# A windowed attention block on one core: the last denominators' rows go first, VectorE copies the shift rows, ScalarE issues them later

## The reference

```
h   = layer_norm(x) padded to 28 x 28, cut in 14 x 14 windows (4 an image)
q, k, v = heads of h @ qkv_w + qkv_b              # 12 heads of 16
s   = (q * 16**-0.5) @ k.T + q @ Rh.T (rows) + q @ Rw.T (columns)
o   = softmax(s) @ v;  o = o @ proj_w + proj_b
x2  = x + o                                       # windows put back, padding cut off
h2  = layer_norm(x2)
out = x2 + gelu(h2 @ mlp_w1 + mlp_b1) @ mlp_w2 + mlp_b2
```

## Time and profile before

| | |
|---|---|
| median of 3 runs | 262.92 us (262.45 to 263.22) |
| the profiled execution | 264.93 us, span 263.1 us, mean granted clock 0.981 |
| TensorE busy | 242.9 us (92%), 1996 matmuls |
| weight loads | 189.6 us (72%) |
| VectorE busy | 166.4 us (63%) |
| ScalarE busy | 133.5 us (51%) |
| GpSimd busy | 115.5 us (44%) |
| chain that ended last | PE 61%, DVE 12%, ACT 9%, DMA 8%, issue 3% |

### The profile page before, as it was taken

One profiled execution on the slowest core, in us unless ns is written; L12 is line 12 of the kernel. 1 busy time (PEld: TensorE's weight loads), 2 busy tenths in 40 slices (PEclk: granted clock), 3 DMA queues, 4 the chain that ended last, 5 costly groups with the idle time before them and its releaser, 6 DMA issues.

```text
span 263.1 us, 5440 instructions
## 1 busy us (share of the span) xinstructions
PE 242.9 (92%) x1996; PEld 189.6 (72%) x1996; DVE 166.4 (63%) x453; ACT 133.5 (51%) x240; POOL 115.5 (44%) x180
## 2 busy tenths in 40 slices
PE   7789999999799998999999998949999999999994
PEld 3335578897677776778776765638878889798994
DVE  3997739237878887888879895627996461400010
ACT  2156698336557675676756666520357461604100
POOL 4449775905017665857566772910410490000000
PEclk9999999999799999999999999976999999999999
DMA  5745224786047778676767624371000001000011
GB/s 173 184 110 136 50 58 111 184 200 157 25 116 157 167 183 194 155 170 169 191 165 187 163 54 140 95 235 47 0 2 2 0 0 60 2 30 30 20 43 60
DMA packets 22232, 27.80 MB, mean 106 GB/s; under 512 B 7288, under 2 KB 18410, under 8 KB 22206
## 3 DMA queue, kind: packets, MB, share of 16 engines
q1 hardware_dynamic: 18253, 21.37, 31.0%
q0 software_dynamic: 3424, 5.89, 10.0%
q10 hardware_dynamic: 528, 0.20, 0.3%
HBM read 5.84 MB, written 1.57 MB: 28 GB/s over the span
## 4 chain that ended last, share of the span: by engine, by line
PE 61%; DVE 12%; ACT 9%; DMA 8%; issue 3%; ACTq 2%; POOL 2%; SPq 1%; DVEq 0%; POOLq 0%
PE ps L1472 12%; PE ps L1456 8%; PE ps L1246 6%; PE ps L1312 5%; PE ps L1288 5%; PE ps L1137 5%; DMA kop<-hl 3%; ACT pm L744 3%; DVE bias L931 3%; PE ps L1211 2%; PE ps L1369 2%; PE ps L1356 2%; PE ps L1317 2%; ACTq L724 2%; DMA ot<-osb 2%
## 5 line engine op out<-in xcount | busy, mean ns | idle before, releaser
L950 DVE TENSOR_REDUCE nmax<-ps 98x2 f32<-98x392 f32 x96 | 52.8, 565 | 19.0 <-PE ps L1246 17.3
L744 ACT ACTIVATE pm<-ps 98x784 f32<-98x784 f32 x48 | 39.0, 825 | 16.2 <-PE ps L1288 16.1
L1246 PE MATMUL ps<-kop,qop 126*98 126x196 f32 x192 | 37.3, 279 | 2.3 <-DVE nmax L950 0.9
L1246 PEld LDWEIGHTS ps<-kop,qop 126*98 126x98 f32 x192 | 25.8, 168 | 9.3 <-DVE nmax L950 4.0
L1472 PE MATMUL ps<-w2t,gl 128*128 128x192 f32 x192 | 31.7, 326 | 0.0
L1472 PEld LDWEIGHTS ps<-w2t,gl 128*128 128x128 f32 x192 | 31.4, 190 | 0.3
L816 ACT ACTIVATE gl<-ps,vec 128x512 f32<-128x512 f32 x24 | 16.1, 684 | 29.4 <-PE ps L1456 29.4
L1288 PE MATMUL ps<-qop,kop 128*98 128x196 f32 x192 | 26.6, 262 | 0.0
L1093 DVE TENSOR_TENSOR xn<-ps,xres 128x384 f32<-128x384 f32 x8 | 4.5, 558 | 33.5 <-PE ps L1472 33.5
L955 DVE TENSOR_REDUCE nmax<-ps 120x1 f32<-120x316 f32 x48 | 22.2, 482 | 4.0 <-PE ps L1252 3.0
L1137 PE MATMUL ps<-ht,bias 128*128 128x512 f32 x48 | 21.6, 595 | 2.7 <-DVE ht L866 1.4
(11 more groups left out here) (162 smaller groups left out, 499.1 us busy)
## 6 DMA issues: line engine op xcount, KB each, us to landing
qop<-bias POOLq DMA_DIRECT2D x7, 343.0 KB, 5.7
qop<-hl SPq DMA_DIRECT2D x12, 196.0 KB
kop<-hl SPq DMA_DIRECT2D x12, 196.0 KB
bias<-in_x SPq DMA_DIRECT2D x4, 384.0 KB, 4.6
xres<-in_x SPq DMA_DIRECT2D x4, 384.0 KB, 4.2
out<-xn SPq DMA_DIRECT2D x8, 192.0 KB, 1.9
kop<-kst SPq DMA_DIRECT2D x3, 477.8 KB
ot<-osb POOLq DMA_DIRECT2D x44, 32.0 KB, 2.3
```

The source lines that it names most:

```text
L744: a.activation(pm[0:HALF, gi], ps[0:HALF, b0:b0 + 2, 0:2 * WIN], ACT.Exp).then_inc(s["exp_done"], 1)
L950: v_.tensor_reduce(nmax[0:HALF, h % 2, 2 * n:2 * n + 2], ps[0:HALF, bank, 0:2 * WIN].rearrange("p (t k) -> p t k", t=2), AX.X, ALU.max, ne ...
L1246: o = mm(ps[0:HALF, bank, WIN * t:WIN * (t + 1)], q[0:R_MAX, WIN * n + HALF * t:WIN * n + HALF * (t + 1)], kk[0:R_MAX, WIN * n:WIN * (n + ...
```

## The change

Seven edits:

- SyncE issues the load of the residual's first chunk after the two DMAs of the last denominators' rows, no longer before.
- GpSimd waits for the last reciprocals before it splits the first MLP layer's weights.
- The copies of the shift rows out of PSUM move from ScalarE to VectorE: the main one after the tenth reduction of the head, the rest one after the second reduction of the next head (for the last head after the loop).
- ScalarE keeps only the DMAs of the shift rows, and issues them after the exponentials of groups 3 and 5, no longer before those of groups 3 and 5.
- VectorE forms the last reciprocals before the fourth multiply of heads 0 to 7.
- TensorE's first two projections change places.
- In the second norm's eviction ScalarE does both banks without waiting for VectorE, and VectorE follows it bank by bank; the next transposes wait for VectorE's reads and no longer for its low parts.

```diff
-            load_residual(0)
             sp.wait_ge(s["rden_ready"], 3)
             for l in range(2):
                 sp.dma_start(rd[4 * l:4 * (l + 1), 1].bitcast(F32), den_parts[:, 2, l]).then_inc(s["rd1_in"], 16)
+            load_residual(0)
             load_residual(1)
...
                 pool.wait_ge(*loaded)
+                pool.wait_ge(s["rden_ready"], 3)
                 g.tensor_copy(high[:], w[:]).then_inc(s["w1_split"], 1)
...
-            def main_shifts(h):
-
-                act.wait_ge(s["mt_done"], 2 * h + 1)
-                if h >= 2:
-                    act.wait_ge(shift_in[h % 2], 16 * (h // 2))
-                a.copy(shift[:, h % 2].bitcast(F32R), ps[0:4 * B, score_bank(main_max_use(h)), 0:HALF]).then_inc(s["shift_ready"], 1)
+            def store_main_shifts(h):
+
                 act.wait_ge(s["shift_ready"], 2 * h + 1)
                 act.dma_start(qop[h % RING].bitcast(F32)[R_MAX:ROWS, 0:MAIN], shift[:, h % 2]).then_inc(shift_in[h % 2], 16)
...
-                    if gi == (10 - LEAD) // 2 and h + 1 < HEADS:
-                        main_shifts(h + 1)
-                    if gi == (14 - LEAD) // 2 and h + 1 < HEADS:
-                        rest_shifts(h + 1)
+                    if gi == 3 and h + 1 < HEADS:
+                        store_main_shifts(h + 1)
+                    if gi == 5 and h + 1 < HEADS:
+                        store_rest_shifts(h + 1)
...
                 act.wait_ge(s["tp2_done"], 2 * c + 2)
-                act.wait_ge(s["h2f_ready"], 2 * c + 1)
                 a.activation(h2s[0:C - P, c % 2], ps[0:C - P, 7, :], ACT.Identity, scale=vec[0:C - P, G2B:G2B + 1],
...
+            def main_shifts(h):
+
+                dve.wait_ge(s["mt_done"], 2 * h + 1)
+                if h >= 2:
+                    dve.wait_ge(shift_in[h % 2], 16 * (h // 2))
+                v_.tensor_copy(shift[:, h % 2].bitcast(F32R), ps[0:4 * B, score_bank(main_max_use(h)), 0:HALF]
+                               ).then_inc(s["shift_ready"], 1)
...
                     maxima(h, n)
+                    if n == 1 and h:
+                        rest_shifts(h - 1)
...
                     maxima(h, n)
+                    if n == 9:
+                        main_shifts(h)
...
                     reciprocal_parts(k)
+            rest_shifts(LAST)
...
-            for j in range(4):
+            for j in range(3):
                 normalise(0, j)
             for par in range(2):
                 dve.wait_ge(o_in[par], 5 * 16 * (LAST // 2))
             dve.wait_ge(s["ten_den_in"], 16)
             reciprocal_parts(2)
+            normalise(0, 3)
...
-                dve.wait_ge(s["tp2_done"], 2 * c + 2)
-                v_.tensor_scalar(h2g[:], ps[0:C - P, 7, :], vec[0:C - P, G2B:G2B + 1], vec[0:C - P, B2B:B2B + 1],
-                                 ALU.mult, ALU.add).then_inc(s["h2f_ready"], 1)
                 dve.wait_ge(s["h2h_ready"], 2 * c + 1)
                 v_.tensor_scalar(h2f[:], ps[:, 6, :], vec[:, G2A:G2A + 1], vec[:, B2A:B2A + 1],
+                                 ALU.mult, ALU.add).then_inc(s["h2f_ready"], 1)
+                dve.wait_ge(s["h2h_ready"], 2 * c + 2)
+                v_.tensor_scalar(h2g[:], ps[0:C - P, 7, :], vec[0:C - P, G2B:G2B + 1], vec[0:C - P, B2B:B2B + 1],
                                  ALU.mult, ALU.add).then_inc(s["h2f_ready"], 1)
...
                         elif gi == 4:
+                            projection_of_eight(1)
+                        else:
                             projection_of_eight(0)
-                        else:
-                            projection_of_eight(1)
...
                     pe.wait_ge(s["h2h_ready"], 2 * c)
-                    pe.wait_ge(s["h2l_ready"], 2 * c)
+                    pe.wait_ge(s["h2f_ready"], 2 * c)
```

More of the change, by code:

```diff
@@ L715, in _, with store_rest_shifts @@
                 last_bias_columns(b)
-            def main_shifts(h):
-                act.wait_ge(s["mt_done"], 2 * h + 1)
-                if h >= 2:
-                    act.wait_ge(shift_in[h % 2], 16 * (h // 2))
-                a.copy(shift[:, h % 2].bitcast(F32R), ps[0:4 * B, score_bank(main_max_use(h)), 0:HALF]).then_inc(s["shift_ready"], 1)
+            def store_main_shifts(h):
                 act.wait_ge(s["shift_ready"], 2 * h + 1)
                 act.dma_start(qop[h % RING].bitcast(F32)[R_MAX:ROWS, 0:MAIN], shift[:, h % 2]).then_inc(shift_in[h % 2], 16)
[L726 to L731, removed]
+            def store_rest_shifts(h):
                 act.wait_ge(s["shift_ready"], 2 * h + 2)
@@ L757, in output @@
                 a.copy(osb[:, h % 2], ps[:, 6, :]).then_inc(s["osb_ready"], 1)
-            main_shifts(0)
-            rest_shifts(0)
+            store_main_shifts(0)
+            store_rest_shifts(0)
             a.activation(warm[:, 4:8], warm[:, 0:4], ACT.Exp)
@@ L962, in maxima_parts, with rest_shifts @@
                 v_.tensor_tensor(low.bitcast(F32R), m, high, ALU.subtract).then_inc(s["parts_ready"], 1)
+            def main_shifts(h):
[4 more added lines that the diff above has]
+                               ).then_inc(s["shift_ready"], 1)
+            def rest_shifts(h):
+                dve.wait_ge(s["mt_done"], 2 * h + 2)
+                if h >= 2:
+                    dve.wait_ge(rest_shift_in[h % 2], 16 * (h // 2))
+                v_.tensor_copy(shift_rest[:, h % 2].bitcast(F32R), ps[0:2 * NP, score_bank(rest_max_use(h)), 0:PAIR]
+                               ).then_inc(s["shift_ready"], 1)
             def reciprocal_parts(k):
@@ L1084, in second_channels_lo @@
                 v_.tensor_tensor(h2l[:, c % 2], h2f[:], h2h[:, c % 2], ALU.subtract).then_inc(s["h2l_ready"], 1)
-                dve.wait_ge(s["h2h_ready"], 2 * c + 2)
                 v_.tensor_tensor(h2s[C - P:P, c % 2], h2g[:], h2s[0:C - P, c % 2],
```

## The result

The changed kernel takes 260.53 us (median of 7 runs, 258.71 to 261.9), the kernel before on the same chip 263.22 (7 runs): ratio 0.9893, 95% interval 0.9854 to 0.9932. That is 2.7 us less where 5.4 were forecast. The profiled execution took 261.90 us with a span of 260.1 (264.93 and 263.1 before), mean granted clock 0.974.

The account below looks back on a forecast made before the run. TensorE was taken to lead, pausing 3.3 us for the last denominators, after which the clock fell, and once per head. Denominators 4.1 + heads 1.3 = 5.4 off 262.9 gave 257.5 us; 8 in 10 between 255.9 and 260.9.

Parts of the forecast that it names:

- Denominators: Way of the last denominators to the MLP: 4.1 us saved, 2.2 by earlier rows and 1.9 by the clock.
- the residual's place: Residual's first load issued behind the two stores of rows: price 0, at the other end 1.0 us.
- the splits are hidden: GpSimd's later weight splits end some 5.3 us after 168.0, are read at 192.06, and cost nothing.
- after about 2.4 us: Head 10's denominators, sent off at 164.00, land about 2.4 us later, in time for the earlier reciprocals.
- the 0.9 for the reordering: Last reciprocals before VectorE's fourth multiply of the first eight heads: gain 0.9 us.
- Shift copies, stores: In the heads: VectorE copies 0.25 us each; group 3's exponentials start at 124.41, shift DMA issued under them.
- slower: Rival: later shifts take 3.84 us to landing, each of 11 heads starts weights 0.81 to 0.85 later; 267.8 us, chance 0.07.
- What the heads give: Pauses before group 3's sums, 3.1 us over the heads, of which 1.3 us were counted as arriving.
- the clock should then stay up: After TensorE's pause near 171 us, cut to 1.1 us, the granted clock holds: 1.9 us gained.
- the clock still falls: Rival: clock falls after the 1.1 us pause and thin spread matmuls; 2.2 + 1.3 saved, 259.4 us, chance 0.16.
- threshold of 3.36 us: Shift's time to landing from which the later shifts in the heads make the kernel slower.
- Second norm: ScalarE evicts without waiting for VectorE, whose four instructions keep their total: price 0, without a later wait 0.8 us.

Follow-up runs that it names:

- e15: The denominators' edits alone on the kernel before, but with the residual's first load at its old place ahead of the rows' stores; 259.49 us, ratio 0.9858.
- e9: The kernel before with the denominators' edits alone, same as e1, measured again on another chip; 259.11 us, ratio 0.9817.
- e1: The kernel before with the diff's lines on the denominators alone, no shift edits and old evictions; 259.10 us, ratio 0.9836.
- e10: The kernel before with the denominators' edits and the second norm's evictions, no shift edits; 258.97 us, ratio 0.9816.
- e18: e10 again, measured on the chip of e17; 259.61 us, ratio 0.9848.
- e14: e1 without GpSimd's wait for the last reciprocals before splitting the weights; 262.37 us, ratio 0.9962.
- e8: The changed kernel with the first MLP layer's weight loads moved up, behind the denominator rows of the first eight heads; 260.44 us, ratio 0.9908.
- e11: e1 with two idle 128x512 matmuls in TensorE's pause ahead of the last spread matmul; 259.28 us, ratio 0.9821.
- e16: e10 with one idle 128x512 matmul in TensorE's pause behind the last sums; 259.73 us, ratio 0.9866.
- e3: The changed kernel with four idle 128x512 matmuls in TensorE's pause ahead of the last spread matmul; 261.26 us, ratio 0.9926.
- e5: The changed kernel itself, measured again; 260.42 us, ratio 0.9901.
- e6: The changed kernel with the second norm's evictions and the transposes' wait as before; 260.77 us, ratio 0.9905.
- e13: The changed kernel with two idle 128x512 matmuls in TensorE's pause behind the last sums; 259.52 us, ratio 0.9861.
- e4: The changed kernel with the first MLP weights' loads moved behind the last rows' stores and the residual's first load; 260.63 us, ratio 0.9905.
- e17: e1 with VectorE's shift copies, both shift stores at their old places in ScalarE's program; 261.09 us, ratio 0.9886.
- e12: The kernel before with three idle 128x512 matmuls in TensorE's pause and no edit of the change; 261.29 us, ratio 0.9897.
- e7: The changed kernel with ScalarE issuing the main shifts behind the exponentials of group 2 instead of group 3; 260.91 us, ratio 0.9890.

## Why the prediction came out 3 us low

*Denominators: right in sum, wrong in two prices.* The cast and subtraction are 0.20 and 0.23, the residual's place costs nothing that can be told (e15 against e9), the splits are hidden, and e1 gives 4.2 us where 4.1 were forecast. So the whole miss lies with the shift edits: forecast at 1.3 gained, they cost 1.4. In the profiled execution of e10 the rows go out 3.97 us after head 10's store (forecast 4.0), and the pause is 1.10 (forecast 1.1). The first wrong price is the clock's: kept, it is worth 2.4 us and not 1.9, but e1's executions did not all keep it, so that 4.2 meets 4.1 is in part luck. The second is the landing of head 10's store, "after about 2.4 us". That is the median of eleven; for this very store the trace of before has 3.18 us from issue to landing, for the ten others 1.85 to 2.54. With the old shift stores VectorE still waited for it in e9 and e18 (0.25 and 0.46). One attribution is in doubt: in e14's profile the rows of the 0.9 for the reordering are not there without GpSimd's wait, though its median is 0.9 below the kernel before. What its rows do show is the lock. The Trainium skill's page "SBUF — State Buffer", section "Who interferes with whom", has the loser wait for the whole instruction; e14's ends within 0.05 and 0.10 of GpSimd's agree.

*Shift copies, stores: right as events.* 0.25 each, and the issue runs under the exponentials. Their landing was not: see "slower" below.

*The step that failed: "What the heads give", 1.3 us counted as arriving.* The heads did get shorter. From the issue of head 0's store of denominators to the start of TensorE's last sums the old heads take 89.5 to 90.3 us in eight executions (mean 89.9; e14, with a wait of its own there, left out), those with all shift edits 88.6 to 89.8 in seven (mean 89.2; e8 left out). The profile of before has 90.5, with the 0.76 of head 3 that none of these fifteen shows again (at most 0.30 there). So 0.7 us are won and not 1.3: the pauses saved come back in part as waits for the shift's DMA (0.55 and 0.38) and for VectorE (0.70 and 0.75 in heads 8 and 9, where e10 has 0.36 and 0.55). And what is won does not arrive, because TensorE's next wait is for the last rows, which by the same measure are issued only 0.1 sooner (means of 87.0 in the seven profiles with the denominators' edits alone or with evictions, e1, e9, e10, e11, e15, e16 and e18, and 86.9 in the changed kernel, e3, e5, e6 and e13). The last main shift now goes out 5.00 us ahead of head 10's store instead of 5.73; SyncE, which waits for its landing, sends the first layer's weights 2.79 ahead of that store instead of 3.58, and the store, taken to land "in time", keeps VectorE waiting until 3.2 to 3.8 us behind its issue (the reciprocal starts 2.9 to 3.4 behind it with the old stores, not always after a wait). With those loads moved away (e4) it was there within 2.63.

*And "the clock should then stay up" with it.* The pause grew to 1.78, 1.93 and 2.36 in the three profiles with the late store and nothing in the pause (changed, e5, e6), and in these the clock fell, for all of the stretch or half of it; after 0.94, 1.01, 1.10, 1.37, 1.39 and 1.44 it held, after 1.34 (e1) and 1.41 (e17) it fell for a part. So a shorter pause makes a fall less likely, but its length alone doesn't settle it. The sum for the profiled execution is then: TensorE resumes 2.8 earlier instead of 2.2 + 1.3 = 3.5, and the clock gives nothing instead of 1.9 (in truth 2.4, e12), 2.8 in all. That is the mechanism of the rival "the clock still falls", which had 0.16; its 259.4 still counted the 1.3 us of the heads and is 1.1 below the median measured. Over executions it is a mixture: 7 of 29 of the kernels without shift edits (e1, e9, e10, e15, e18) have a mean clock of 1.00 and none 0.981 or less, of 25 with them (changed, e5, e6) one and five; their means are 259.3 and 260.7. That is a hint only, for the mean clock also holds a fall near 70 us, which 14 of the 20 profiles have (69.7 to 73.1 in the changed kernel's), e9 and e18 among them, whose clock held behind the last spread matmul.

*Slower: not so, but by the issue and not by the landing.* Its threshold of 3.36 us was passed. In the changed kernel's profile the shift issued at 123.26 was waited for until 127.45, 4.19 us later, the one of 131.90 until 135.91; by the semaphores' records nine of the twelve main shifts landed 3.4 to 4.1 us after their issue, where those of the kernel before took 2.1 to 2.9 and those of e7, issued one group of exponentials earlier, 2.2 to 2.8. What kept this cheap is that the issue runs under the exponentials, so only heads 7 and 8 waited. What holds the late shifts up was not tested. Behind the weights in e8 the same mechanism cost 2.15 us once. *Second norm: 0,* as forecast (e6, e10).

*Still open* is whether the pause explains all of the 1.4 us. e13 says so within its interval. But e7 and e17, whose first layer's weights go out 3.55 to 3.57 ahead of the store and whose pauses are short, are at 260.9 and 261.1 too, though their last rows go out 0.2 and 0.6 us later behind head 0's store than in e1's kind. Some of the price may belong to VectorE's copies; no run here settles it.

The best version measured is the denominators' edits without the shift edits, with or without the evictions: 258.97 to 259.61 in e1, e9, e10 and e18, 0.9 to 1.6 us below the changed kernel.

## What to carry to other kernels

A saving ahead of a wait counts only if what ends that wait moves with it; so ask of each saving which event TensorE waits for next: here TensorE came 0.7 us sooner to rows that were paced by a store and the transfers around it, and most of that turned into pause. Where a pause of TensorE brings the clock down, price it by filling it with idle matmuls (2.5 us here) before trusting a sum that leaves a short one. When two edits attack one instruction, take each out alone. And take a transfer's time from the row of that very transfer: the median of eleven stores, 2.4 us, hid the 3.18 of the one that mattered.

## What the runs showed of the hardware

The lock that held the cast in e14 seems to work in head 9 too. GpSimd fills `on` with eight memsets of 0.49 us, and the cast behind head 9's reciprocals takes from 0.20 to 0.97 us depending on where these fall. In the 16 profiles in which it is longer than 0.20, it ends 0.05 or 0.06 us after one of the memsets, and not always the first: in e16 it begins in one that ends at 152.17 and ends at 152.68, behind the next (152.63). Here e18, where they begin after it, and e16, where they begin just before it (start, us; VectorE's row, then GpSimd's; first e18, then e16):

```profile
151.47 0.20 DVE L968 CAST kst<-den 128x64 fp32r<-128x64 f32 x1
...
151.75 3.89 POOL L593 MEMSET on<- 32x512 f32 x8 [1.52 <-DMA kop<-hl]
```

```profile
151.71 0.97 DVE L968 CAST kst<-den 128x64 fp32r<-128x64 f32 x1
...
151.65 3.94 POOL L593 MEMSET on<- 32x512 f32 x8 [1.18 <-DMA kop<-hl]
```

TensorE's wait for VectorE that follows is 0.24 in e18 and 1.01 in e16, so this can be a part of the scatter of one kernel between executions. A row of a single profile is such a draw; the wait of 0.76 in the earlier trace rows, for a DMA, was another.
